# The product with the values behind both pairs of a slot, and three expert pieces a slot at the end

## What is computed

```
x  = L0_attn_x                                  # (4, 512, 128)
xn = _layernorm(x, axis=-1)
x  = x + _L0_attn_ref(xn, ...) + _L0_ffn_ref(xn, ...)
xn = _layernorm(x, axis=-1)
x  = x + _L1_attn_ref(xn, ...) + _L1_ffn_ref(xn, ...)

# attention, each head
scores = jnp.einsum('bhqd,bhkd->bhqk', q, k) / math.sqrt(HEAD_DIM)
scores = jnp.where(mask[None, None], scores, -1e9)          # layer 1
out    = jnp.einsum('bhqk,bhkd->bhqd', softmax(scores), v) @ Wo.T + bo

# experts of layer 1: comb has the two chosen weights of each token
for e in range(E):
    g = jax.nn.silu(xf @ gate_proj_w[e].T)
    u = xf @ up_proj_w[e].T
    out = out + comb[:, e:e + 1] * (g * u @ down_proj_w[e].T)
```

## Time and profile before

| | us |
|---|---|
| runs | 545.46, 543.98, 542.29; median 543.98 |
| the profiled execution | 544.03 |
| its span, first to last instruction | 542.0 |
| granted TensorE clock, mean | 0.95 of 2.4 GHz |
| PE busy | 454.8 (84%), 3394 matmuls |
| DVE busy | 400.5 (74%) |
| ACT busy | 328.8 (61%) |
| POOL busy | 262.5 (48%) |

### The profile page before, as it was taken

One profiled execution on the slowest core, in us unless ns is written; L12 is line 12 of the kernel. 1 busy time (PEld: TensorE's weight loads), 2 busy tenths in 40 slices (PEclk: granted clock), 3 DMA queues, 4 the chain that ended last, 5 costly groups with the idle time before them and its releaser, 6 DMA issues.

```text
span 542.0 us, 9302 instructions
## 1 busy us (share of the span) xinstructions
PE 454.8 (84%) x3394; PEld 169.4 (31%) x3394; DVE 400.5 (74%) x538; ACT 328.8 (61%) x422; POOL 262.5 (48%) x499
## 2 busy tenths in 40 slices
PE   3456979889988999899989898987899999999952
PEld 1101213224322433242312431221245453455511
DVE  5699778886998699869887798789876777623204
ACT  2102666776677667656676577777766567667560
POOL 6861263724425562886378657884201233163240
PEclk9755889999999999999999999999999999999995
DMA  3896596244511360626252645174731111010018
GB/s 82 238 230 89 89 343 106 93 163 146 90 43 61 118 62 4 66 72 127 25 52 39 157 43 56 41 160 68 109 52 32 45 50 50 4 44 25 21 47 219
DMA packets 143742, 48.27 MB, mean 89 GB/s; under 512 B 109890, under 2 KB 139090, under 8 KB 142866
## 3 DMA queue, kind: packets, MB, share of 16 engines
q1 hardware_dynamic: 141394, 42.93, 38.1%
q0 software_dynamic: 2304, 4.76, 2.6%
HBM read 22.81 MB, written 23.14 MB: 85 GB/s over the span
## 4 chain that ended last, share of the span: by engine, by line
PE 53%; DVE 18%; issue 10%; ACT 10%; DMA 4%; SPq 4%; POOL 1%; POOLq 0%; ACTq 0%; DVEq 0%
PE ps L763 14%; DVE mx L1114 11%; PE ps L747 9%; PE ps L732 7%; ACT PT L962 6%; PE ps L802 3%; PE ps L810 3%; PE ps L785 2%; PE ps L803 2%; SPq L433 2%; PE ps L693 2%; PE ps L825 2%; PE ps L822 2%; PE ps L786 1%; DVE th L1135 1%
## 5 line engine op out<-in xcount | busy, mean ns | idle before, releaser
L1114 DVE TENSOR_REDUCE mx<-ps 128x2 f32<-128x1024 f32 x256 | 309.4, 1223 | 73.1 <-PE ps L732 65.1
L962 ACT ACTIVATE PT<-ps 128x1024 f32<-128x1024 f32 x256 | 258.6, 1026 | 125.9 <-PE ps L747 116.5
L763 PE MATMUL ps<-PT,Vp 128*32 128x512 f32 x1024 | 138.1, 611 | 5.4 <-ACT PT L962 4.4
L732 PE MATMUL ps<-KO,QO 48*128 48x512 bf16 (+1 forms) x512 | 104.5, 406 | 39.7 <-ACT PT L962 22.6
L747 PE MATMUL ps<-QO,KO 59*128 59x512 bf16 x512 | 100.2, 390 | 3.8 <-DMA QO<-mT 2.5
L520 POOL DMA_INDIRECT y_tokens<-expert_io,meta x40 | 38.6, 964 | 71.5 <-ACT expert_io L994 48.5
L747 PEld LDWEIGHTS ps<-QO,KO 59*128 59x128 bf16 x512 | 24.6, 93 | 142.8 <-issue 87.9
L1135 DVE SCALAR_TENSOR_TENSOR th<-th,ps 128x320 f32<-128x320 f32 (+1 forms) x44 | 23.8, 541 | 35.2 <-ACT th L978 29.4
L732 PEld LDWEIGHTS ps<-KO,QO 48*128 48x128 bf16 (+1 forms) x512 | 25.6, 96 | 70.9 <-ACT PT L962 38.6
L545 POOL CAST mp<-mx 128x32 bf16<-128x32 f32 x16 | 3.4, 214 | 82.9 <-DVE mx L1114 78.7
L509 POOL DMA_INDIRECT x_places<-xe,place_i x32 | 31.9, 995 | 22.3 <-ACT PT L962 15.2
(11 more groups left out here) (166 smaller groups left out, 475.1 us busy)
## 6 DMA issues: line engine op xcount, KB each, us to landing
z<-part SPq DMA_DIRECT2D x16, 384.0 KB
z<-part SPq DMA_DIRECT2D x16, 256.0 KB
QO<-z SPq DMA_DIRECT2D x64, 48.0 KB
KO<-z SPq DMA_DIRECT2D x64, 48.0 KB
x_places<-expert_io SPq DMA_DIRECT2D x2, 1300.0 KB, 7.4
expert_io<-x_places SPq DMA_DIRECT2D x8, 320.0 KB, 3.5
QO<-z SPq DMA_DIRECT2D x6, 384.0 KB
KO<-z SPq DMA_DIRECT2D x6, 384.0 KB
```

Source lines behind the costliest of these rows:

```text
L732: mm = pe.matmul(ps[:, 2 * pair + half, :], rows_of(QO[u % 3], half, 2 * s + jj, rows, (qt, qt + 1)), rows_of(KO[u % 3], half, 2 * s + jj, ...
L763: last = pe.matmul(ps[32 * g:32 * g + 32, PV_BANK, :], Vp[u % 2][:, k, head(s, g), :], PT[:, (2 * t + g % 2) % 4, g // 2, :], start=(s % 2 ...
L962: act.activation(PT[:, e % 4], ps[:, 2 * pair:2 * pair + 2, :], ACT.Exp).then_inc(exp_done, 1)
L1114: dve.tensor_reduce(mx[:, a, qt, col:col + 5:4], ps[:, 2 * pair:2 * pair + 2, :], AX_X, ALU.max, negate=True).then_inc(max_read, 1)
```

## The change

V moves on PE behind S1 and M1. In unit 7 from slot 4 on, a slot takes three expert pieces in place of two, so the last comes in slot 9; `result_slot` follows. DVE adds the results of the first sequence ahead of the last normalisation. The three DMAs of the experts' weights leave the list `loads`: two are issued in `sync_unit` of unit 0, between the writes of z and the reads, the third in unit 1 at the same place; they have a semaphore of their own. ACT's and POOL's code is as before, but for what `expert_work_at` and `result_slot` give.

```
+            t, two = SLOTS_U * (u - (U - 2)) + slot - EXPERTS_FROM, SLOTS_U + (PAIRS_U - LEAD) // 2 - EXPERTS_FROM
+            if t < 0:
+                return []
+            a = 2 * t if t < two else 3 * t - two
+            return expert_work[a:a + 2 + (t >= two)]
...
+            return next(SLOTS_U * u + slot for u in range(U - 2, U) for slot in range(SLOTS_U)
+                        if ("expert", e) in expert_work_at(u, slot))
...
                 operand_writes(sp, p, 1)
+                if u < 2:
+                    for dst, src in expert_loads[0:2] if u == 0 else expert_loads[2:3]:
+                        sp.dma_start(dst, src).then_inc(experts_loaded, 16)
...
-            pe.wait_ge(loaded, N_LOAD)
+            pe.wait_ge(experts_loaded, N_EXPERT)
...
                 if maxima:
                     max_mms(pe, maxima[0])
-                if u > 0 or slot > 0:
-                    value_mms(pe, SLOTS_U * u + slot - 1)
                 if slot == 6 and u >= 1:
                     pe.wait_ge(mT_ready, 2 * u + 2)
                     out_mms(pe, u - 1, (0, 1))
                 score_mms(pe, u, slot, 1)
                 if maxima:
                     max_mms(pe, maxima[1])
+                if u > 0 or slot > 0:
+                    value_mms(pe, SLOTS_U * u + slot - 1)
...
         def last_vector(dve):
+            add_results(dve, 0)
             normalize_out(dve, U - 1, 1)
-            for b in range(B):
+            for b in range(1, B):
                 add_results(dve, b)
```

More of the change, by code:

```diff
@@ L169, in build @@
         loaded = sem("loaded")
+        experts_loaded = sem("experts_loaded")
         x_loaded = [sem(f"x_loaded{b}") for b in range(B)]
@@ L299, in expert_work_at @@
         def expert_work_at(u, slot):
-            a = 2 * (SLOTS_U * (u - (U - 2)) + slot - EXPERTS_FROM)
-            return expert_work[a:a + 2] if a >= 0 else []
+            t, two = SLOTS_U * (u - (U - 2)) + slot - EXPERTS_FROM, SLOTS_U + (PAIRS_U - LEAD) // 2 - EXPERTS_FROM
[3 more added lines that the diff above has]
+            return expert_work[a:a + 2 + (t >= two)]
         def result_slot(e):
-            return SLOTS_U * (U - 2) + EXPERTS_FROM + expert_work.index(("expert", e)) // 2
+            return next(SLOTS_U * u + slot for u in range(U - 2, U) for slot in range(SLOTS_U)
+                        if ("expert", e) in expert_work_at(u, slot))
         taken = [("max", q) for q in range(LEAD)]
@@ L1228, in build @@
                  (w_proj[1][:], wo[1]), (b_proj[1][:], bo[1][None, :].to_broadcast([P, D])),
-                 (w_router[:], router_T), (eg[:], eg_T), (eu[:], eu_T),
-                 (ed[:], ed_T.rearrange("e (b p) d -> p e b d", p=P))]
-        N_LOAD, N_FIRST = 16 * len(loads), 16 * len(first_loads)
+                 (w_router[:], router_T)]
+        expert_loads = [(eg[:], eg_T), (eu[:], eu_T), (ed[:], ed_T.rearrange("e (b p) d -> p e b d", p=P))]
+        N_LOAD, N_EXPERT, N_FIRST = 16 * len(loads), 16 * len(expert_loads), 16 * len(first_loads)
         def load_x(sp, b):
```

## The result

The changed kernel takes 580.25 us (median of 4 runs, 579.08 to 583.53) against 544.16 (4 runs, 542.29 to 545.46) for the kernel before: ratio 1.068, 95% interval 1.062 to 1.073. The forecast was 582.6 us, slower. The profiled execution took 580.82 us with a span of 578.5.

A forecast was written before the change was run, and what follows sets the result against it. TensorE was taken as busiest, its waits for exponentials deciding; V last exposes 0.83 us a slot. Terms +29.1, +4.9, +9.5, −3.4 and −1.5 sum to +38.6 on 544.0: 582.6 us, range 569 to 593.

The forecast's parts named there:

- M1's wait: Slots with maxima: the second maxima product waits 0.83 us for the exponential of its own slot's first scores, nothing passing.
- S0 to S0: Time between first score products of successive slots: 2.82 us plus all side work of the slot.
- Units 1 to 5: Main stretch: 229.8 us of PE work plus 71.3 of waits, 301.1 against 272.0, so +29.1 us.
- Unit 6 with four slots: Unit 6 and the first four slots of unit 7: 103.9 against 94.4 us, +9.5.
- Unit 0: First unit: 60.9 against 56.0 us, +4.9, with about 2 us of slot 8's DMA wait already taken off.
- The last twelve slots: Unit 7 from slot 4, no maxima: exponentials back to back, 0.92 us apart; 48.7 against 52.1 us, −3.4.
- The tail: After the last exponential: load issued at −0.2, first addition at +5.9, residual at 12.6 against 14.1 us, −1.5.
- The check on the waits: Sign to look for: maxima products wait some 90 us for ACT instead of 61, in some 110 slots.
- A wait partly covered: Rival: the wait is 0.68 instead of 0.83 us a slot, 17 us less in sum, 565 us; chance 0.09.
- Faster: Rival: second maxima product not held by its own slot's first exponential; 539 us; chance of faster or equal 0.05.
- The end: Rival: three-piece slots and the earlier load bring nothing at the kernel's end, 587.5 us; chance 0.05.
- The clock: Rival: granted clock falls from 2.4 to 1.2 GHz in unit 5, its work about doubles, 622 us; chance 0.03.

The follow-up runs named there:

- v_alone: Kernel before with only the value products (V) moved behind the second scores and second maxima products: 582.52 us, ratio 1.080.
- loads_alone: Kernel before with only the later loads of the experts' weights: 540.90 us, ratio 0.995.
- mixed2: Changed kernel, value products back between first maxima and second scores where a slot has maxima and in unit 7's slot 6; first addition behind normalisation: 536.50 us, 0.987.
- after_again: The changed kernel, unaltered, measured again on another chip: 578.47 us, ratio 1.072 to the kernel before.
- v_ahead_m1: Changed kernel with the value products one place earlier, behind the second scores but ahead of the second maxima product: 556.77 us, ratio 1.033.
- three_alone: Kernel before with only the three expert pieces a slot in the last unit once no maxima are left: 541.97 us, ratio 0.995.
- after: The changed kernel with all parts of the change, against the kernel before: 580.25 us, ratio 1.068.
- mixed: Changed kernel with value products back between first maxima and second scores wherever a slot has maxima, last only in the last twelve slots: 532.48 us, 0.987.
- v_ahead_m1_alone: Kernel before with only the value products moved behind the second scores and ahead of the second maxima product: 561.91 us, ratio 1.041.
- rest: Changed kernel with the value products back between first maxima and second scores in every slot: 531.20 us, ratio 0.984.

## Why the prediction was right

**The mechanism and its size.** M1's wait is 0.84 where 0.83 was said, S0 to S0 is 2.83 in slots 0, 14 and 15 (2.82), slot 6's wait is 1.35 (1.4), and v_alone and the halved exponential show the cause. Units 1 to 5: +27.3 for +29.1. The own work was counted right; what is over came mostly from slots 5 and 13 (3.03 where the walk's terms give 3.13) and slot 1 (3.61 for 3.72): V and the small side products of these slots cover some 0.1 more than I gave them. Unit 2 took 62.7 (62.8 said), unit 5 53.5 (53.9). Unit 6 with four slots: 103.87 for 103.9, as said.

**Unit 0** was +2.6 for +4.9. I put this down to an error in the walk and not in the mechanism, one slot of 2.8 us counted twice (without it the walk gives 58.1, and 58.55 was measured); the steps of this walk are not written out in the prediction, so that is not shown. That the later loads cost nothing elsewhere held. But the 2 us that they were to take off the wait of slot 8 do not arise in this order: v_alone, with the early loads, had 0.15 of that wait and 57.97 us in unit 0. The 3.5 us of loads_alone are a gain of the old order only.

**The last twelve slots** were +0.8 for −3.4. Three things were missing. Slot 6 took 10.55 us where it takes 7.96 with V ahead (mixed2): 1.0 of that is the longer wait for mT's copy, which the walk had, and 1.6 is V, the gates and what ran with them at the lower clock, which it had not. In slot 5 (5.87; 5.14 in after_again) S1 stood 0.67 behind the copy of a result on ACT. And ACT's halt put 1.06, then 0.35 and 0.54 us of idle time between the last exponentials, where I had eleven of them back to back. None of the three comes in every execution: after_again, without the last two, had 49.9 (−2.1), and v_ahead_m1, with the same instructions and none of them, 48.27 (−3.8). So the walk fits a profile in which nothing disturbs these slots; what it left out is that something often does.

**The tail** was −3.6 for −1.5, the other side of the same coin. The load was issued at 562.39, 2.2 ahead of the end of the last exponential (564.60) instead of 0.2; it landed by 568.41, 6.0 later, as 6.1 was said. The first addition came at +3.8 for +5.9, and the residual 6.7 behind it, as said. The halt of ACT moved the last exponential and not the load. Last slots and tail together were −2.8 for −4.9 (−5.2 in v_ahead_m1): the results' way back, not the exponentials, sets this sum. The load was issued 50.67 us behind the start of slot 4, for 48.35 in v_ahead_m1; slot 6 (1.6) and slot 5 (0.7) make up these 2.3.

**How good the total is.** It is 2.3 us off, and the terms are less good than that: 1.8 and 2.3 too much in units 1 to 5 and unit 0, 4.2 too little in the last slots, 2.1 too much in the tail. That they cancel to 2 us is in part luck; the 27 us of the middle, which decide the sign and the size, are not.

**The check on the waits** of "some 90 us for ACT instead of 61" was a misreading: 156.7 us, in a view that counts the weight load's and the product's wait apart. The step used 0.83 from starts and was not touched by it, but as a test I had set it badly. In program the waits are 103, for the 110 said.

**The rivals.** A wait partly covered (0.68 a slot, 565) would have shown in the plain slots; they are 2.83. "Faster" is out: M1 is held by its own S0's exponential, as the halved exponential shows. The end did something in the changed kernel, though little. The clock did stay at 1.00 in units 1 to 6 with PE idle in each slot, so that rival is out where it would have cost 40 us; in this profile it came true in one slot, where I had not looked, and at the end. The earlier trace rows said that the clock holds at 5.14 busy of 9 us; three_alone shows the same work losing it. The Trainium skill (TensorE: Matmul & The Clock Gate, A second HAM failure mode: psum-queue depth-cycling) warns of a fall by short idles between groups of matmuls; the 100 waits of 0.84 in units 1 to 6 do not bear it out here, and slot 6 and three_alone fit it without showing what is needed (v_ahead_m1 has the same slot 6 at 1.00). The rule of the Trainium skill that matmuls start in program order (PSUM — Partial Sum Buffer, Engine vs sequencer instructions) held: in no slot read did V pass the waiting M1. The slot shown from 230.87 is a test of it: V's exponentials were over at 230.86, and it still started 0.32 behind M1, at 232.69. What the prediction took for agreement, M0's wait ahead of V in the earlier trace rows, is no test, because V waits there for the same exponential as M0.

## What to carry to other kernels

When work on an in-order engine is moved, ask what wait it stood in front of: V looked like one more product between two others, and was the 1.0 us that hid a 0.84 us wait in a hundred slots. With three pairs of banks in turn, write down for each product whose reader it waits for, walk each order once round, and compare the loops (2.82, 2.82, 3.03 here); a loop of the same length may still be worse, if all side work now comes on top of it. Gains behind the main loop are only worth what the last arrival lets through, here the results' way back by DMA.

## What the runs showed of the hardware

- The granted clock fell to the 1.2 GHz level in slot 6 of unit 7 in three profiles (after, after_again, mixed), each time after PE had stood 1.57 us. In three others (v_alone and v_ahead_m1_alone, V 1.07; v_ahead_m1, V 1.06) PE stood 1.57 us in the same slot and the clock stayed at 1.00. The first two have two pieces in it; v_ahead_m1 has three, and the same instructions as the three in which the clock fell. So the number of pieces does not tell them apart; what does is open.
- The same code kept the clock (rest, slots of 2.51 us) or lost it (three_alone's profile, 3.59), worth some 4 us of 540.
- ScalarE, in a row of exponentials that start 0.90 us apart and take 1.02 each, stood still for 1.05 to 1.06 us once in two of the profiles (after: 559.72, mixed2: 515.95), both times ahead of the first exponential of slot 14 and with the products that it reads begun 1.8 us before; in after_again, mixed and v_ahead_m1 twelve ran without a gap. Its cause was not tried.
- Units 1 to 5 of the old order took 268.2 us in both profiles from one chip (rest, mixed) and 271.8 to 272.3 in four from another, the difference standing in a few slots (slot 5 of unit 5: 2.45 against 3.0 to 3.2; slot 8 of unit 4: 3.9 to 4.1 against 4.3 to 4.6). No wait of PE for a DMA goes with it: in the kernel before ACT and DVE both started 1.3 to 1.5 us late at the head of slot 5 of unit 4 (291.66 and 291.70), on scores and maxima products issued by 290.25. The cause is open; with V last they took 298.6 on two chips.
